# Quarter side's chain six positions later, and the last batch's second norm, scores and records in two halves of four tiles

## The reference, cut to what matters

```python
# softmax attention of layer 1: 16 heads of 8, causal, with a temperature per row
sim = einsum('bhid,bhjd->bhij', q, k) / sqrt(8)          # causal mask
p = softmax(sim); entropy = -sum(p * log(p + 1e-9))
beta = where(entropy > 0.5, max(poly(entropy), 1), 1)
x = x + (softmax(sim * beta) @ v) @ Wo.T + bo
# balanced experts of layer 1
feat = layernorm(x).reshape(-1, 128)                     # kept as "feats"
norm = layer_norm(feat) * ln_g + ln_b                    # a second norm of the same rows
scores = norm @ centroids.T                              # 4096 tokens x 8 experts
order = balanced_assignment(scores)                      # needs all scores
```

## Time and profile before

| | us |
|---|---|
| median of 3 runs | 2200.9 |
| lowest and highest | 2197.46, 2201.28 |
| the profiled execution's own time | 2206.78 |
| its span, from the first to the last instruction | 2205.0 |
| TensorE, VectorE, ScalarE busy | 1635.4, 1478.1, 1395.2 |

### The profile page before, as it was taken

The page is one execution under the profiler, slowest core; times in us unless marked ns, Lnnn a source line. Parts: engine busy times, 40 slices in busy tenths (PEclk is TensorE's granted clock), DMA queues, the critical chain, the costliest instruction groups (busy, mean ns, idle before and its releaser), DMA issues. The chain is left out here.

```text
span 2205.0 us, 22468 instructions
## 1 busy us (share of the span) xinstructions
PE 1635.4 (74%) x6426; PEld 696.5 (32%) x6426; DVE 1478.1 (67%) x3532; ACT 1395.2 (63%) x2633; POOL 142.3 (6%) x126
## 2 busy tenths in 40 slices
PE   4787899999999744777778877778778789611157
PEld 2443344444444201232223322223222233301144
DVE  6646343544463699888887788887878875359942
ACT  3554443434333498989989999898999988400012
POOL 0000000000000100000000000000000000026446
PEclk9898899999999855576766656666665558755568
DMA  4000065454546300111101011110110102260022
GB/s 148 0 0 0 2 165 153 129 157 130 152 124 190 90 32 31 55 62 43 49 34 62 33 38 43 46 62 28 36 44 23 62 30 61 59 153 0 1 84 70
DMA packets 56912, 147.81 MB, mean 67 GB/s; under 512 B 7788, under 2 KB 22508, under 8 KB 54180
## 3 DMA queue, kind: packets, MB, share of 16 engines
q1 hardware_dynamic: 52564, 137.07, 20.7%
q0 software_dynamic: 3072, 8.39, 1.2%
q10 hardware_dynamic: 1152, 0.92, 0.3%
HBM read 126.38 MB, written 19.97 MB: 66 GB/s over the span
## 5 line engine op out<-in xcount | busy, mean ns | idle before, releaser
L1729 DVE CUSTOM_DVE_ANT_0 sa_e<-sa_ps,sa_mask 128x1024 f32<-128x1024 f32 (+7 forms) x512 | 386.1, 754 | 112.2 <-PE sa_ps L1469 105.0
L1469 PE MATMUL sa_ps<-sa_space 72*128 72x512 bf16 (+3 forms) x768 | 299.7, 461 | 188.8 <-DVE sa_nmax L1729 141.8
L1738 DVE CUSTOM_DVE_ANT_0 sa_lg<-sa_e,sa_lg 128x1024 f32<-128x1024 f32 (+7 forms) x512 | 386.5, 755 | 62.2 <-ACT sa_lg L1622 61.8
L1612 ACT ACTIVATE sa_e<-sa_e,sa_nmax 128x1024 f32<-128x1024 f32 (+7 forms) x512 | 406.0, 793 | 22.0 <-DVE sa_nmax L1729 21.0
L1622 ACT ACTIVATE sa_lg<-sa_e,sa_sum 128x1024 f32<-128x1024 f32 (+7 forms) x512 | 405.0, 791 | 5.8 <-DVE sa_prod L1738 5.5
L1630 ACT ACTIVATE sa_p<-sa_ps 128x512 f32<-128x512 f32 x576 | 337.9, 609 | 68.0 <-PE sa_ps L1519 49.5
L875 ACT ACTIVATE mx_h<-mx_ps 128x512 f32<-128x512 f32 (+1 forms) x264 | 157.0, 597 | 276.2 <-PE mx_ps L800 255.6
L974 DVE TENSOR_TENSOR mx_hw<-mx_spread,mx_h 128x512 f32<-128x512 f32 x256 | 176.2, 691 | 231.5 <-PE mx_ps L813 192.6
L1519 PE MATMUL sa_ps<-sa_q2s,sa_k2s 75*128 75x512 bf16 (+3 forms) x768 | 299.0, 435 | 34.1 <-ACT sa_p L1630 28.5
L800 PE MATMUL mx_ps<-mx_f,m 128*128 128x512 f32 x512 | 262.2, 598 | 0.8 <-ACT mx_h L875 0.8
L813 PE MATMUL mx_ps<-mx_hw,m 128*128 128x512 f32 x512 | 260.0, 595 | 0.0
(11 more groups left out here) (326 smaller groups left out, 1852.2 us busy)
## 6 DMA issues: line engine op xcount, KB each, us to landing
mx_spread<-mx_spill SPq DMA_DIRECT2D x256, 256.0 KB, 4.0
sa_space<-sa_spill_q SPq DMA_DIRECT2D x96, 96.0 KB
sa_space<-sa_spill_k SPq DMA_DIRECT2D x96, 96.0 KB
sa_k2s<-sa_spill_k SPq DMA_DIRECT2D x48, 192.0 KB
sa_q2s<-sa_spill_q SPq DMA_DIRECT2D x48, 192.0 KB
m<-m_in SPq DMA_DIRECT2D x1, 4256.0 KB, 18.5
records<-sa_e SPq DMA_DIRECT2D x8, 512.0 KB, 5.9
be_w<-w_in SPq DMA_DIRECT2D x16, 256.0 KB, 11.9
```

The source lines that it names most:

```text
L1469: last = nc.tensor.matmul(out[:, col:col + w], q_ring[:, c % 2, local, i * P:(i + 1) * P], k_ring[:, c % 2, local, col:col + w], start=Tru ...
L1612: nc.scalar.activation(e[:, u % 5, 0:w], e[:, u % 5, 0:w], ACT.Exp, scale=-1.0, bias=nmax[:, b % 2, i, h:h + 1], accum_out=sums[:, b % 2, ...
L1729: nc.vector.tensor_tensor_reduce(out=e[:, u % 5, 0:w], in0=slot_of("unit", u)[:, 0:w], in1=mask_wide[:, SEQ - w:SEQ], scale=1.0, scalar=3. ...
L1738: nc.vector.tensor_tensor_reduce(out=lg[:, u % 2, 0:w], in0=e[:, u % 5, 0:w], in1=lg[:, u % 2, 0:w], scale=1.0, scalar=0.0, op0=ALU.mult, ...
```

## The change

The quarter side's wides go from 485 and 487 to 491 and 493, its shift from 489 to 495, the parts of its q from 488 to 491 to 494 to 497, and SP's spill from 490 to 496. The other sides stay.

The last batch's `sc` chain becomes two parts, p = 3 and 4, of four tiles each, that start at positions 616 and 618. Each of its instructions works on four tiles; its three records DMAs and its scores DMA are halved as well. For these two parts the transposes go to `both` and the scores to two other banks, with a wait for all of `exp2`. In all batches the two small products of the left variance are issued ahead of the scaling, no longer behind it.

```diff
-LAST_SCORES = FIRST2 + ALL1 + 20
-END = LAST_SCORES + SCORES_STEP
+LAST_SCORES = FIRST2 + ALL1 + 18
+SCORE_PARTS = [*((b, slice(0, TILES)) for b in range(BATCH - 1)),
+               (BATCH - 1, slice(0, TILES // 2)), (BATCH - 1, slice(TILES // 2, TILES))]
+SCORE_STARTS = [*(SCORES_FROM + SCORES_STEP * b for b in range(BATCH - 1)), LAST_SCORES, LAST_SCORES + 2]
+END = LAST_SCORES + 2 + SCORES_STEP
...
-        WIDE_AT, SHIFT_AT = (5, 7), 9
+        def wide_at(k):
+            return (11, 13) if k == SPLIT else (5, 7)
+        def shift_at(k):
+            return 15 if k == SPLIT else 9
+        def spilled_at(u):
+            for k, end in enumerate(SIDE_ENDS):
+                if u - end == wide_at(k)[1] + 3:
+                    return k
+            return None
+        def parted_at(u):
+            for k, end in enumerate(SIDE_ENDS):
+                r = u - end - wide_at(k)[1]
+                if 1 <= r <= 4:
+                    return k, ((0,), (1,), (2, 3), (4,))[r - 1]
+            return None, ()
...
-                    if (b := scores_at(u, 14)) is not None:
-                        sp.wait_ge(normed.sem, b + 1)
-                        some = slice(b * TILES, (b + 1) * TILES)
-                        for k, rows in enumerate((tiles_of(norms[b % 2]), x[:, some, :], tiles_of(feats[b % 2]))):
+                    if (p := scores_at(u, 14)) is not None:
+                        b, ts = SCORE_PARTS[p]
+                        sp.wait_ge(normed.sem, p + 1)
+                        some = slice(b * TILES + ts.start, b * TILES + ts.stop)
+                        for k, rows in enumerate((tiles_of(norms[b % 2])[:, ts, :], x[:, some, :],
+                                                  tiles_of(feats[b % 2])[:, ts, :])):
                             sp.dma_start(records_v[:, some, k, :], rows).then_inc(kept[b % 2], 16)
...
+                def score_experts(p):
+                    pe.wait_ge(n_ready.sem, p + 1)
+                    if is_whole(p):
+                        out = take_slot("score", p)
+                    else:
+                        pe.wait_ge(exp2_ready.sem, GROUP * ALL2)
+                        out = flat(2)
+                    for col in range(cols_of(p).start, cols_of(p).stop, BANK):
...
+                def total(p):
+                    b, ts = SCORE_PARTS[p]
+                    dve.wait_ge(x_ready.sem, 2 * b + 2 * ts.stop // TILES)
+                    nc.vector.reduce_sum(sums_of[:, ts], seq(b)[:, ts, :], axis=AX.X).then_inc(summed.sem, 1)
...
+                def scale_rows(p):
+                    b, ts = SCORE_PARTS[p]
+                    if b >= 2 and not of_half(p):
+                        dve.wait_ge(kept[b % 2], 16 * KINDS * (b // 2))
+                    dve.wait_ge(rooted.sem, p + 1)
+                    link(nc.vector.tensor_tensor(left_var[:, ts], var_of[:, ts], rstd_of[:, ts], ALU.mult))
+                    nc.vector.tensor_tensor(left_var[:, ts], left_var[:, ts], rstd_of[:, ts], ALU.mult
+                                            ).then_inc(left_ready.sem, 1)
+                    nc.vector.tensor_tensor(tiles_of(feats[b % 2])[:, ts, :], cent_of[:, ts, :], wide(rstd_of, ts), ALU.mult
+                                            ).then_inc(scaled.sem, 1)
```

More of the change, by code:

```diff
@@ L1197, in scores_at @@
 def scores_at(u, r):
-    for b in range(BATCH):
-        if u - r == (SCORES_FROM + SCORES_STEP * b if b + 1 < BATCH else LAST_SCORES):
-            return b
-    return None
+    return SCORE_STARTS.index(u - r) if u - r in SCORE_STARTS else None
 def query_part(spill, a, side, heads):
@@ L1293, in softmax_attention_block, with of_half, is_whole, whole_part @@
         half_tiles = (slice(0, TILES // 2), slice(TILES // 2, TILES))
+        def of_half(p):
+            return SCORE_PARTS[p][1].start > 0
+        def is_whole(p):
+            return SCORE_PARTS[p][0] < BATCH - 1
+        def whole_part(u, r):
+            p = scores_at(u, r)
+            return p if p is not None and is_whole(p) else None
+        def cols_of(p):
+            ts = SCORE_PARTS[p][1]
+            return slice(ts.start * P, ts.stop * P)
         def slot_uses():
@@ L1489, in turn_shift, with turn_normed @@
                     last.then_inc(shift_t.sem, 1)
-                def turn_normed(b):
-                    pe.wait_ge(normed.sem, b + 1)
-                    out = tiles_of(take_slot("norm", b))
-                    for t in range(TILES):
+                def turn_normed(p):
+                    b, ts = SCORE_PARTS[p]
+                    pe.wait_ge(normed.sem, p + 1)
+                    out = tiles_of(take_slot("norm", p) if is_whole(p) else both)
+                    for t in range(TILES)[ts]:
                         last = nc.tensor.transpose(out[:, t, :], tiles_of(norms[b % 2])[:, t, :], ident)
                     last.then_inc(n_t.sem, 1)
-                def score_experts(b):
-                    pe.wait_ge(n_ready.sem, b + 1)
-                    out = take_slot("score", b)
-                    for n in range(HALVES):
-                        cols = slice(n * BANK, (n + 1) * BANK)
+                def score_experts(p):
[6 more added lines that the diff above has]
+                    for col in range(cols_of(p).start, cols_of(p).stop, BANK):
+                        cols = slice(col, col + BANK)
                         last = nc.tensor.matmul(out[0:E1, cols], mat(m4, MATS4, "cent1"), n_cm[:, cols],
@@ L1593, in _ @@
                         out_project(i)
-                    if (b := scores_at(u, 15)) is not None:
-                        turn_normed(b)
-                    if (b := scores_at(u, 18)) is not None:
-                        score_experts(b)
+                    if (p := scores_at(u, 15)) is not None:
+                        turn_normed(p)
+                    if (p := scores_at(u, 18)) is not None:
+                        score_experts(p)
                     for m in pieces2_at(u + 1):
@@ new lines, in affine, with take_scores @@
+                def affine(p):
+                    cols = cols_of(p)
+                    act.wait_ge(n_t.sem, p + 1)
+                    if p and not of_half(p):
+                        act.wait_ge(score_mm.sem, p)
+                    out = slot_of("norm", p) if is_whole(p) else both
+                    nc.scalar.activation(n_cm[:, cols], out[:, cols], ACT.Identity, bias=vec(vecs, "ln_b"),
+                                         scale=vec(vecs, "ln_g")).then_inc(n_ready.sem, 1)
+                def take_scores(p):
+                    cols = cols_of(p)
+                    act.wait_ge(score_mm.sem, p + 1)
+                    if p and not of_half(p):
+                        act.wait_ge(scored.sem, 16 * p)
+                    out = slot_of("score", p) if is_whole(p) else flat(2)
+                    nc.scalar.activation(score_sb[:, cols], out[0:E1, cols], ACT.Copy).then_inc(score_ready.sem, 1)
@@ new lines, in wide, with centre @@
+                def wide(v, ts):
+                    return v[:, ts].unsqueeze(2).broadcast_to([P, ts.stop - ts.start, CH])
+                def centre(p):
+                    b, ts = SCORE_PARTS[p]
+                    dve.wait_ge(summed.sem, p + 1)
+                    nc.vector.scalar_tensor_tensor(out=cent_of[:, ts, :], in0=wide(sums_of, ts), scalar=-1.0 / CH,
+                                                   in1=seq(b)[:, ts, :], op0=ALU.mult, op1=ALU.add
+                                                   ).then_inc(centred.sem, 1)
@@ L1875, in add_bias, with norm_again @@
+                def norm_again(p):
+                    b, ts = SCORE_PARTS[p]
+                    if b >= 2:
+                        dve.wait_ge(n_t.sem, b - 1)
+                    dve.wait_ge(scaled.sem, p + 1)
+                    dve.wait_ge(root_left.sem, p + 1)
+                    nc.vector.tensor_tensor(tiles_of(norms[b % 2])[:, ts, :], tiles_of(feats[b % 2])[:, ts, :],
+                                            wide(left_rstd, ts), ALU.mult).then_inc(normed.sem, 1)
                 def add_bias(b):
@@ L2350, in _ @@
                 for n in range(2):
-                    pool.wait_ge(kept[n], 16 * KINDS * BATCH // 2)
+                    pool.wait_ge(kept[n], 16 * KINDS * sum(b % 2 == n for b, _ in SCORE_PARTS))
                 for e in range(AHEAD_ROWS):
```

136 lines of the change are left out of this document (71 added, 65 removed).

## The result

The changed kernel took 2192.62 us (median of 17 runs, 2185.32 to 2199.49), the kernel before 2203.01 in the same series (17 runs, 2195.51 to 2206.5). The ratio is 0.9949, 95% interval 0.994 to 0.9959: 11.2 us faster, from 9.0 to 13.2. The forecast was 10.1 us faster and 2190.8.

The account below looks back on a forecast made before the run. ScalarE's exponentials and logarithms set the pace, idling 15.49 us around the quarter side, and the tail is a chain across engines. Quarter side -5.3 and tail -4.75 sum to -10.05 us: 2190.8 from 2200.9, range 2185 to 2198.

Parts of the forecast that it names:

- Positions 485 to 490: Softmax attention: without paired guests the stretch falls from 26.37 us to batch 1's 17.06, 9.31 us less.
- What comes back: Positions 491 to 497: moved guests cost 4.0 us, one late evacuation 2.95 plus the shift's 1.01; ends 2.59 and 15.
- The tail: Last output projection to store of scores: halves let the last store issue at 1933.7, not 1938.55; 4.75 us after slack.
- the score passes: TensorE in the tail: four passes take 3.45 us, a half's two 1.73, ending at 1931.3 and 1933.1.
- The slack of the records: Tail: records out by 1933.8, last store's data 0.9 after its issue; no loss but little slack, 0.1 us taken off.
- D: Rival, tail: half-size records move at half the rate, 11 us, so the tail gives nothing; 2195.6 us, chance 0.04.
- the sign: Tail, sign of wrongness: records still moving when the last store's data go.
- B: Rival, quarter side: the stall moves with the chain, its move gives 0 to 1 us; 2195.7, chance 0.17.
- C: Rival, 1840 to 1880: shifted phases leave TensorE's low clock, 1.7 us a group; 2208 at ten groups, chance 0.08.
- E: Rival, more gain: quarter side pays back only 2.6 us and tail gives 5.6; 2188.6, chance 0.13.
- part 1: Quarter side six positions later: -9.3 + 4.0 = -5.3 us, ends -6.7 and +5.7.

Follow-up runs that it names:

- projections_moved: Kernel before, quarter side unmoved, third batch's attended halves and output projections eight positions later; ratio 0.9976.
- shift_left: The changed kernel with the quarter side's wides moved but its shift left at 489; ratio 0.9957.
- change_again: The changed kernel itself, unedited, in another execution; ratio to the kernel before 0.9943.
- tail_only: The changed kernel with the quarter side's wides and shift back at their old positions; ratio to the kernel before 0.9977.
- quarter_ten_later: The changed kernel with the quarter side ten positions later, not six (wides 495 and 497, shift 499); ratio 0.9943.
- banks_apart: The changed kernel; last batch's attended halves and projections take `both` without the hand-round, its bias added earlier; ratio 0.9925.
- banks_and_projections: banks_apart with the third batch's projections eight positions later in place of the quarter side's move; ratio 0.9917.
- x_records_early: The changed kernel with the x part of the last batch's records sent right after each half's `finish`; ratio 0.9955.
- the part alone: Kernel before with only the quarter side's wides, shift, split parts and spill six positions later, tail as before; ratio 0.9978.
- products_first: Kernel before with only the two small products of the left variance ahead of the scaling; one run, 2204.36 us.

## Why the prediction was right, step by step

**Positions 485 to 490.** Forecast -9.3, from 26.37 to batch 1's 17.06. Measured 15.97, 15.98 and 16.27 in three kernels: -10.4 or -10.1 against that 26.37, and -9.4 or -9.1 against the 25.39 and 25.40 of two more executions without the move. The cause, two guests of `both` in one position, is shown from both sides (projections_moved, shift_left).

**What comes back.** Forecast +4.0, measured +3.8 in six executions and +6.4 in one. Here the size was right by luck and the mechanism wrong. I had ScalarE reach position 491 with nothing in hand and pay for a late evacuation with idle time. The same stretch (the evacuation that opens 491 to that of unit 511) in the kernel before:

```profile
1787.65:1820.64 32.99, 28.57 (x142) 10.31 (x142) 27.22 (x73) 31.91 (x67) 0.00 (x0) 0.55 0.15 49
```

ScalarE idles 1.1 us in it, and in the change 36.79 - 35.02 = 1.8: only 0.7 more. What has grown is its work, from 31.91 us to 35.02, while in 485 to 490 that fell from 14.53 to 11.75. The edges of these stretches are instructions of VectorE; with the stall gone VectorE opens 491 sooner, and ScalarE carries some 3 us of its work over that edge. So about 3 us of the -10.4 come back in the +3.8 as the same work on the other side of an edge, and only the two together mean something: in 480 to 507 ScalarE idles 8.6 us instead of 15.5, and the stretch is 6.6 us shorter (5.6 against the two other executions), where 5.3 was forecast. Real starvation shows in change_again, 4.2 us idle in the stretch, most of it `exp2` waiting for score pieces at the lower clock; the forecast had no term for that clock.

**The tail.** Forecast -4.75, measured -5.7 here and in tail_only. `norm_again` of the two halves was forecast to end 6.44 and 7.04 us after the start of `finish(7)`; it ends at 6.35 and 6.95 (1904.17 to 1910.52 and 1911.12). The mis-sized term is the score passes: I took 3.45 for four, at the low clock. They took 2.76, 0.69 less, because the clock rose in the middle of them. The eight transposes also follow one another, done after 8.37 instead of 8.59. This makes the last store 0.95 earlier than forecast, after 11.79 instead of 12.74. In four halved kernels (shift_left, quarter_ten_later, banks_apart, banks_and_projections) the four passes took 3.32 to 3.58, nearly all at the low clock, as I had it, and the last store came after 12.34 to 12.61, close to the forecast; their tails are still 5.3 to 5.6 us shorter than the 20.75.

"TensorE: Matmul & The Clock Gate" of the Trainium skill, section What's actually happening, has the low clock as the default, lifted by activity. The grant of 0.50, 0.82 and then 1.00 during the denser tail agrees with it; in the sparser tail of before the four passes took their 3.45 at 0.50, and the grant rose to 0.89 only around their end. In quarter_ten_later the tail is as dense as in the change up to the passes, and all four ran at 0.50, so when the rise comes is not set by the tail alone.

**The slack of the records.** I took 0.1 off for it, and from the last store to the load it is 3.26 us in the change against 3.16 before: 0.1. But this is two errors that cancel. A last store of half the size with the records out of its way needs 2.83 (x_records_early, and the four kernels with a late last store), so 0.33 should have been gained; and the records cost 0.43, not 0.1. I let them end at 1933.8 of the old times, 12.8 us after the start of `finish(7)`, and 0.8 ahead of the last store's data. They end 13.0 after it (1917.16, by the share of 0.16 in the last window), close to that sum. But the last store came earlier than forecast, so the slack was gone. D's mechanism, and the sign that I had named for it, are there; its price rested on half the rate, and the rate is 285 GB/s, as with the whole ones.

**The sum.** -5.3 - 4.75 = -10.05 against -11.2 (-9.0 to -13.2) by the ratio, and -12.3 by stretches of one pair of profiles. The middle's first two errors add to 1.3 and the tail's is 0.95; execution-to-execution differences are as large. The 2.1 us behind position 509 stand in neither sum. That the total came so close is therefore in part luck.

**The rivals.** B falls: the stall did not go along with the chain, ScalarE's idle time from 480 to 495 fell to 7.8 us with the shift at its end, and the part alone gives 4.9 us. C did not come in its place: it named the forty microseconds from 1840 of the old times. The changed kernel is some 15 us ahead there, and its grant is 1.00 in the window below, as it is from 1825 to 1865.

```profile
1820.00:1860.00 40.00, 37.34 (x322) 15.63 (x321) 20.26 (x24) 34.36 (x69) 0.00 (x0) 1.00 0.32 97
```

A lower clock went with 2.6 us more in change_again, but behind 490. E's tail (5.6) is what came; its middle (2.6 back) did not.

**Open.** Why the grant in positions 491 to 508 is 0.80 in most executions and 0.66 in one of the same program was not tried; nothing in these kernels sets it. On it hang the 2.6 us there and the 2.1 behind 509, so part 1's worth differs by over 4 us from one execution to another. Not shown either is whether the shared tile or the crowding of TensorE's queue makes a pair dear. And TensorE's longest wait in 480 to 495, 4.0 us ahead of a unit's scores for the copy of an attended half (`sa_attc`), is the same before and after; nothing here touched it.

## What to carry to other kernels

When a shared buffer's guests pair up between two regular uses, move one of the two chains until each position has one guest; here it mattered little which one, and more distance brought nothing. Read the gain over a stretch long enough that no engine carries work over its edge, and check it by the idle time of the engine that sets the pace. In a tail that is one chain across engines, halve the work before reordering it: the halving was worth 5.7 us, the order 0.5. And look for rounds of hand-over that protect a buffer from users who are already gone: here 4.9 us went with it, up to 2.6 of them by a higher clock.

## What the runs showed of the hardware that I had not expected

- The same instructions up to position 480 took 1739.3 to 1750.3 us in these profiled executions, with equal work on VectorE and ScalarE and 15.9 us less on TensorE in the change than in before. A difference of two profiles must be cut into stretches before it is read.
- One and the same program had a granted clock of 0.80 in one execution and 0.66 in another over the same 172 matmuls, which took 25.42 and 31.18 us. In the kernel before a grant of 0.55 or 0.64 over the same stretch made no difference (32.99, 32.98), since ScalarE was busy for 31.91 us of it.
- Two independent 128x512 operations on VectorE start 0.60 us apart though each lasts 0.68 or 0.69 (1904.78, 1905.38 above): the second begins before the first ends.
- Half-size records DMAs are not half as costly to issue: SP took 0.36, 0.51, 1.33 for two, 0.87 and 0.87, 3.9 us for six of 256 KB, where the three of 512 KB in products_first took 0.36, 0.58 and 1.36, 2.3 in all.
- A small store behind 1.57 MB of records on the same queue waited 0.4 us longer to land, and where the last store came early (11.39 to 11.88 us after `finish(7)`), the load came 8.67 to 8.69 us after the first records issue in five kernels.
